# Stores of split weights, gates, x1, x2 and the output issued from GpSimd's queue instead of SyncE's

## The chip, the core and the metric

The kernel runs on one core of one Trainium2 chip. The metric is the device time in microseconds (us) of one execution. A core has TensorE (PE), VectorE (DVE), ScalarE (ACT), GpSimd (POOL) and SyncE (SP), each with its own instruction stream, and sixteen DMA engines that move data for whichever engine issues a transfer.

## The reference

Three residual sub-layers over x of shape 2 x 2048 x 1024 (float32), 4096 tokens in 32 tiles of 128:

```
x = x + 0.5 * ffn(layernorm(x))      # stage 1 (and the prep part of stage 2)
x = x + attn(layernorm(x))           # stage 2
x = x + 0.5 * ffn(layernorm(x))      # stage 3

attn: blocks of 128 tokens; scores of a block against itself and the block before it,
      masked, squared relu, times the values, times w_o
ffn:  thought = layer_norm(x[:, -1]) @ agg_w + agg_b            # last token of each batch only
      4 times: thought += gelu(layer_norm(thought) @ d1_w + d1_b) @ d2_w + d2_b
      broadcast = thought @ bc_w + bc_b
      gate = sigmoid(x @ gate_w + gate_b)                         # every token
      out  = layer_norm(x + gate * broadcast)
```

d1_w is 1024 x 4096 and d2_w 4096 x 1024, so each pass of the "thought" reads 32 MB of weights four times over for only two tokens. Each of the two ffn layers does so.

## The kernel before

All large products run as three float16 products of a high and a low half (a "split"). The order of all work is one list, `PLAN`, made by `whole_plan()`. Every engine has a program that walks the whole list and does its own part of each entry, so all five engines meet the entries in the same order, each at its own pace. An entry whose wait isn't met holds up all later entries on that engine, and only there.

- Stage 1 multiplies q and k weights and v and o weights together ("fold"), splits the gate weights, and computes the gates of all 32 tiles (`plan_gate`). Each gate tile ends in `gate_store`, a store of 512 KB into `gate1_dram` from a ring of 2 buffers, once ScalarE's sigmoid has raised `gated` (line 1356).
- Stage 2 computes x1 (`plan_prep`: norm, add the spread thought, norm, `x1_store` after `prep_stats`, then `prep_low` and the DMA transpose `group_turn`), then queries, values, scores and `collect`, which makes x2; `x2_stores` of a group come at the beginning of the next group's products.
- Stage 3 (`plan_stage_3`) computes gates and the second ffn for all tiles and ends each with `out_store`.
- The thought is a chain of small steps (`Thoughts`, `with_thought`) laid between the products of stage 1 and again of stage 2. Its weights come through ten buffers of 512 KB. `fetch_unit` (lines 836 to 845) issues the load of a unit once what was in the buffer is no longer needed. Some of the d1 and d2 units (64 in all, in both passes) are split into halves on the chip (`t_high` on ScalarE, `t_low` on VectorE, line 1843, which raises `unit_low`), stored to `parts_dram`, and read back from there in later steps (`pair` units).

All transfers are issued by SP. The loop of `sync_program` ends each thought entry with the fetches that hang on it:

```
elif kind == "t_low":
    _, n = a[0].info
    sp.wait_ge(unit_low, n + 1)
    sp.dma_start(parts_dram[...], unit_at(SPLITS[n].slot)).then_inc(parts_out[...], 16)
...
if kind[:2] == "t_":
    for n in a[0].fetch:
        fetch_unit(n)
```

`await_left` (lines 803 to 816), which `fetch_unit` calls, waits for `unit_low` of the same split where the buffer held a unit that was split, and for `unit_used`, raised by PE, in most other cases. POOL only computes the reciprocal square roots of the norms (`rstd`, line 1907, `normalisers`, line 1914) and of the thought (`t_var`, line 1945).

Transfers whose data is read again are guarded by completion semaphores: `x1_out` is waited for by `prep_fetch` (line 964) and `x1_fetch` (line 1002), `gate_out` by `prep_fetch` (line 968), `x2_out` by `x3` (line 1028), `parts_out` by `fetch_unit` and `t_high`, `out_out` by `x3` and the end of SP's program.

Of the kernel before, what the change touches and what calls it, by code (L numbers as in the profile page):

```python
# [14 lines left out]
P = 128  # L15
# [5 lines left out]
HALVES = D // BANK  # L21
# [19 lines left out]
TILE_OF = [b * NT + g * GROUP + i for b, g in GROUP_OF for i in range(GROUP)]  # L41
ORDER_3 = sorted(range(TILES), key=lambda tile: TILE_OF.index(tile) + 5 * (tile % GROUP == 0))
# [562 lines left out]
def macaron_kernel(nc, x, w_attn, w_o, in_gamma, in_beta, agg_w, agg_b, pn_gamma, pn_beta,  # L605
# [179 lines left out]
    def await_out(eng, key):  # L785

        at = BANK_AT[key]
        eng.wait_ge(product_out[at % PRODUCT_BANKS], at // PRODUCT_BANKS + 1)
# [42 lines left out]
    def sync_program():  # L831
# [15 lines left out]
        for kind, *a in PLAN:  # L847
# [56 lines left out]
            elif kind == "x":  # L904
# [3 lines left out]
                elif n:  # L908
                    sp.wait_ge(split_done, SPLIT_AT[("split", "gate", n - 1)] + 1)
                sp.dma_start(x_slots[n % X_RING], x_flat[row_of(TILE_OF[n]), :]).then_inc(x_in[n % X_RING], 16)  # L910
            elif kind == "gate_store":
                n, = a
                sp.wait_ge(gated, n * HALVES + 2)
                sp.dma_start(gate1_dram[row_of(TILE_OF[n]), :], gate_slots[n % GATE_RING]).then_inc(
                    gate_out[n % GATE_RING], 16)
            elif kind == "gate_save":
                k, = a
                sp.wait_ge(split_done, split_total("gate"))
# [4 lines left out]
            elif kind == "t_rows" and a[0].info[0] == 1:  # L923
# [3 lines left out]
                for b in range(B):  # L927
# [3 lines left out]
                    sp.dma_start(t_wide[b * KD:(b + 1) * KD, THOUGHT_ROWS * P:(THOUGHT_ROWS + 1) * P],  # L931
                                 xs_slots[c % XS_RING][P - 1:P, :].rearrange("o (k p) -> o k p", p=P)).then_inc(
                        rows_in, 16)
            elif kind == "t_low":
                _, n = a[0].info
                sp.wait_ge(unit_low, n + 1)
                sp.dma_start(parts_dram[n * P:(n + 1) * P, :], unit_at(SPLITS[n].slot)).then_inc(
                    parts_out[n % len(FOR_SPLITS)], 16)
            elif kind == "t_out":
                t, = a  # L940
                sp.wait_ge(t_dve, t.dve + 1)
                sp.dma_start(row_dram, t_wide[0:B * KD, 0:P]).then_inc(row_out, 16)
            elif kind == "publish":
                tau, = a
                sp.wait_ge(row_out, 16 * (tau + 1))
                if tau:
                    sp.wait_ge(gate_spread, TILES)
                else:
                    for slot in FOR_FIRST:
                        await_left(sp, THOUGHTS.taken[slot])  # L950
                sp.dma_start(thought_row[:, :, :].rearrange("p b d -> p (b d)"),
                             row_dram.rearrange("k p -> (k p)").partition_broadcast(P)).then_inc(thought_row_in, 16)
            elif kind == "prep_fetch":
                n, = a
                for u in (n * GROUP, n * GROUP + 1):
                    s = u % PREP_RING
                    if n == 0:
                        sp.wait_ge(fold_out[s], 16 * (2 * KD // FOLD_RING))
                        sp.wait_ge(split_done, split_total("vo"))
                    else:  # L960
                        sp.wait_ge(x1_out[s], 16 * (u // PREP_RING))
                        sp.wait_ge(h1_ready, u - PREP_RING + 1)
                        sp.wait_ge(y_made, u - PREP_RING + 1)
                    sp.dma_start(px_slots[s], x_flat[row_of(TILE_OF[u]), :]).then_inc(px_in[s], 16)  # L964
                    sp.wait_ge(gate_out[u % GATE_RING], 16 * (u // GATE_RING + 1))
                    if n:
                        sp.wait_ge(group_in[s], 16 * n)
                    sp.dma_start(pg_slots[s], gate1_dram[row_of(TILE_OF[u]), :]).then_inc(pg_in[s], 16)
            elif kind == "group_turn":
                u, = a  # L970
                n, i = divmod(u, GROUP)
                sp.wait_ge(lows_made, u + 1)
                if n >= 4:
                    sp.wait_ge(product_full, BANK_AT[("score", n - 2, 0)] + 1)
                elif n >= 2:
                    sp.wait_ge(product_full, BANK_AT[("gate", TILES - 1, 1)] + 1)
                    sp.wait_ge(gate_saved, 16 * KD)
                else:
                    for slot in FOR_SPLITS:
                        await_left(sp, last_split[0, slot])  # L980
                sp.dma_start_transpose(  # L981
                    group_of(n).rearrange("p h k t -> p (h k) t")[:, :, i * P:(i + 1) * P],
                    pg_slots[u % PREP_RING].bitcast(F16)).then_inc(group_in[i], 16)
            elif kind == "x1_store":
                u, = a
                sp.wait_ge(x1_made, u + 1)
                sp.dma_start(x1_dram[row_of(TILE_OF[u]), :], px_slots[u % PREP_RING]).then_inc(
                    x1_out[u % PREP_RING], 16)
            elif kind == "x1_fetch":
                c, = a  # L990
                s, u = c % XS_RING, COLLECTS[c][1]
                if c < XS_RING:
                    sp.wait_ge(product_full, BANK_AT[("gate", TILES - 1, 1)] + 1)
                    for i in range(GATE_RING):
                        sp.wait_ge(gate_out[i], 16 * len(range(i, TILES, GATE_RING)))
                else:
                    sp.wait_ge(x2_out[s], 16 * (c // XS_RING))
                    sp.wait_ge(moments_made, MOMENT_AT[("x2_stats", c - XS_RING)] + 1)
                    if c - XS_RING in LAST_TOKENS:
                        sp.wait_ge(rows_in, 16 * 2 * B)  # L1000
                sp.wait_ge(x1_out[u % PREP_RING], 16 * (u // PREP_RING + 1))
                sp.dma_start(xs_slots[s], x1_dram[row_of(TILE_OF[u]), :]).then_inc(xs_in[s], 16)
            elif kind == "x2_stores":
                n, = a
                for c, (at, u, _, _) in enumerate(COLLECTS):
                    if at == n:
                        await_out(sp, ("collect", c, 0))
                        await_out(sp, ("collect", c, 1))
                        sp.dma_start(x2_dram[row_of(TILE_OF[u]), :], xs_slots[c % XS_RING]).then_inc(
                            x2_out[c % XS_RING], 16)  # L1010
            elif kind == "load_3":

                sp.wait_ge(product_full, BANK_AT[("q", GROUPS - 1, KD - 2)] + 1)
                sp.wait_ge(gate_saved, 16 * KD)
                sp.dma_start(wide_a[:, :, :].rearrange("p k d -> p (k d)"), gate_pair_dram).then_inc(gate_loaded, 16)
                sp.wait_ge(product_full, BANK_AT[("score", GROUPS - 2, 0)] + 1)
                sp.dma_start(bias_3, gate_b.partition_broadcast(P)).then_inc(bias_in, 16)
            elif kind == "x3":
                n, = a
                s, c = n % X3_RING, COLLECT_OF[TILE_OF.index(ORDER_3[n])]  # L1020
                if n >= X3_RING:
                    sp.wait_ge(out_out[s], 16 * (n // X3_RING))
                elif n < PREP_RING:
                    sp.wait_ge(group_in[n], 16 * GROUPS)
                else:
                    sp.wait_ge(product_full, BANK_AT[("v", GROUPS - 1, 1, 1)] + 1)
                sp.wait_ge(x2_out[c % XS_RING], 16 * (c // XS_RING + 1))
                sp.dma_start(x3_slots[s], x2_dram[row_of(ORDER_3[n]), :]).then_inc(x3_in[s], 16)
            elif kind == "turn_3":
                n, = a  # L1030
                s = n % PAIR3_RING
                sp.wait_ge(lows3_made, n + 1)
                if n >= PAIR3_RING:
                    sp.wait_ge(product_full, BANK_AT[("gate_3", n - PAIR3_RING, 1)] + 1)
                else:
                    await_thoughts(sp)
                sp.dma_start_transpose(as_pair(pair3_slots[s]).rearrange("p h k t -> p (h k) t"),
                                       low3_slots[s].bitcast(F16)).then_inc(pair3_in[s], 16)
            elif kind == "out_store":
                n, = a  # L1040
                sp.wait_ge(ended_3, n + 1)
                sp.dma_start(out_flat[row_of(ORDER_3[n]), :], x3_slots[n % X3_RING]).then_inc(
                    out_out[n % X3_RING], 16)
            if kind[:2] == "t_":
                for n in a[0].fetch:
                    fetch_unit(n)
# [852 lines left out]
    def gpsimd_program():  # L1899
# [16 lines left out]
        for kind, *a in PLAN:  # L1916
            if kind == "start":
# [9 lines left out]
                pool.affine_select(out=identity[:, :], in_=identity[:, :], compare_op=ALU.not_equal, fill=1.0,  # L1927
                                   base=0, pattern=[[-1, P]], channel_multiplier=1).then_inc(constants, 1)
                pool.wait_ge(zeroed, 1)
            elif kind == "norm":  # L1930
                normalisers((kind, a[0]), token_stats[:, TILE_OF[a[0]], :])
            elif kind == "prep_y":
# [44 lines left out]
```

## Time and profile before

| | us |
|---|---|
| median of 3 runs | 2104.67 (2100.16 to 2111.58) |
| profiled execution, its own time | 2108.0 |
| its span, first to last instruction | 2106.8 |
| PE busy | 2012.4 (96%) |
| DVE busy | 1208.6 (57%) |
| ACT busy | 680.0 (32%) |
| POOL busy | 161.8 (8%) |
| mean busy share of the DMA queue that carries all data | 75.9% |

The profile lists busy time by engine, idle time before an instruction with what ended it, and for DMA instructions the time that they hold the issuing queue. "SPq" is SP's queue. TensorE's granted clock was 0.989 of full speed on average. The data moved is 555.78 MB.

### The profile page before, as it was taken

The page shows a single profiled execution, that of the slowest core. Times are in us where ns is not written, and L with a number is a line of the kernel's source. Part 1 is how long each engine was busy: PE and PEld are TensorE (multiplying, and loading weights), DVE is VectorE, ACT ScalarE, POOL GpSimd, SP SyncE. Part 2 cuts the span into 40 slices and gives each one's busy share as a digit, 9 for nine tenths or more (in the row PEclk, how much of TensorE's full clock was granted, in tenths as well). Part 3 has the DMA queues.
Part 4 walks back from the last instruction along what each step waited for, and adds up shares of the span by engine and source line. Part 5 has one row for each costly group of instructions (what it writes and reads, how often), then busy time and mean ns, then how long its engine had stood idle before and what let it go on. Part 6 is the DMA issues. An engine that isn't in the chain of part 4 may idle for free.

```text
span 2106.8 us, 30594 instructions
## 1 busy us (share of the span) xinstructions
PE 2012.4 (96%) x12010; PEld 1026.6 (49%) x12010; DVE 1208.6 (57%) x2152; ACT 680.0 (32%) x947; POOL 161.8 (8%) x278
## 2 busy tenths in 40 slices
PE   8999988998899999998999999999999999999997
PEld 3333433333333347655565556665556564444443
DVE  2323677223533465666766655655555545888887
ACT  0567445212323332223333222111212113444443
POOL 0000000000000010010000000000000001111111
PEclk9999999999999999999999999999999999999999
DMA  8689996878898843358989898898987947555552
GB/s 340 240 324 382 366 326 245 303 272 323 343 399 336 324 154 107 101 152 318 325 289 340 263 318 292 300 350 289 310 287 285 339 161 210 152 154 154 151 150 80
DMA packets 275214, 555.78 MB, mean 264 GB/s; under 512 B 149040, under 2 KB 149248, under 8 KB 274688
## 3 DMA queue, kind: packets, MB, share of 16 engines
q1 hardware_dynamic: 275072, 553.83, 75.9%
q8 instruction: 96, 1.57, 0.3%
q14 instruction: 46, 0.38, 0.0%
HBM read 406.93 MB, written 113.26 MB: 247 GB/s over the span
## 4 chain that ended last, share of the span: by engine, by line
PE 48%; DMA 3%; DVE 2%; SPq 1%; ACT 1%; issue 1%; POOL 0%; ACTq 0%; DVEq 0%
PE product_banks L1060 41%; PE product_banks L1195 3%; PE thought_acc L1260 3%; DMA thought_units<-parts_scratch 1%; DMA gate_arena<-arena 1%; DVE thought_units L1843 0%; SPq L845 0%; SPq L981 0%; DMA thought_units<-in_d_w 0%; PE thought_turn L1268 0%; ACT arena L1376 0%; ACT arena L1379 0%; PE thought_acc L1250 0%; DVE arena L1655 0%; SPq L964 0%
## 5 line engine op out<-in xcount | busy, mean ns | idle before, releaser
L1060 PE MATMUL product_banks<-gate_arena,arena 128*128 128x512 f16 x1536 | 359.3, 386 | 0.0
L1060 PE MATMUL product_banks<-wide_a,thought_units 128*128 128x512 f16 x1536 | 331.7, 379 | 0.0
L1060 PE MATMUL product_banks<-gate_arena,wide_a 128*128 128x256 f16 x2688 | 308.4, 275 | 3.2 <-DMA gate_arena<-arena 3.0
L1060 PE MATMUL product_banks<-wide_b,gate_arena 128*128 128x512 f16 x1344 | 301.8, 379 | 0.0
L1060 PEld LDWEIGHTS product_banks<-gate_arena,wide_a 128*128 128x128 f16 x2688 | 260.9, 99 | 60.6 <-issue 29.7
L1060 PEld LDWEIGHTS product_banks<-gate_arena,arena 128*128 128x128 f16 x1536 | 147.1, 99 | 206.1 <-issue 55.9
L1060 PEld LDWEIGHTS product_banks<-wide_a,thought_units 128*128 128x128 f16 x1536 | 150.3, 98 | 181.6 <-DVE arena L1695 0.3
L1060 PEld LDWEIGHTS product_banks<-wide_b,gate_arena 128*128 128x128 f16 x1344 | 127.1, 98 | 167.6 <-issue 24.9
L1484 DVE BATCH_NORM_STATS2 bn_parts<-arena 128x6 f32<-128x512 f32 x256 | 164.2, 683 | 4.4
L1907 POOL TENSOR_TENSOR token_stats<-stats,minus_half 128x1 f32<-128x1 f32 x96 | 65.7, 684 | 1039.9 <-DVE stats L1492 863.4
L1509 DVE SCALAR_TENSOR_TENSOR arena<-product_banks,inverse_gate,arena 128x512 f32<-128x512 f32 x64 | 47.8, 748 | 166.2 <-PE product_banks L1060 166.1
L1664 DVE SCALAR_TENSOR_TENSOR gate_arena<-product_banks,gate_arena 128x256 f16<-128x256 f32 x128 | 54.1, 423 | 144.5 <-ACT gate_arena L1391 142.2
L1092 PE MATMUL product_banks<-wide_a,wide_b 128*128 128x512 f32 x256 | 121.0, 614 | 6.1 <-DMA wide_a<-in_w_attn 6.0
L1397 ACT ACTIVATE arena<-product_banks,inverse_vo 128x512 f32<-128x512 f32 x64 | 44.0, 687 | 236.8 <-PE product_banks L1060 236.7
L1260 PE MATMUL thought_acc<-thought_units,thought_parts 128*6 128x512 f16 x1328 | 101.2, 381 | 19.9 <-DMA thought_units<-parts_scratch 13.7
L1195 PE MATMUL product_banks<-arena,key_weights 128*128 128x512 f32 x248 | 112.8, 600 | 6.9 <-issue 3.2
L1907 POOL TENSOR_TENSOR stats<-stats,minus_half 128x1 f32<-128x1 f32 x64 | 64.2, 1003 | 700.8 <-DVE stats L1492 416.3
L1368 ACT ACTIVATE arena<-arena,token_stats 128x1024 f32<-128x1024 f32 x32 | 39.5, 1236 | 230.7 <-DMA arena<-in_x 230.7
L1391 ACT ACTIVATE gate_arena<-product_banks 128x256 f16<-128x256 f32 x128 | 41.5, 379 | 211.5 <-PE product_banks L1060 211.5
L1425 ACT ACTIVATE arena<-arena 128x512 f32<-128x512 f32 x64 | 40.3, 630 | 175.5 <-DVE arena L1509 175.5
L1655 DVE SCALAR_TENSOR_TENSOR arena<-arena 128x1024 f16<-128x1024 f32 x32 | 39.2, 1224 | 96.3 <-ACT arena L1379 96.1
L1092 PEld LDWEIGHTS product_banks<-wide_a,wide_b 128*128 128x128 f32 x256 | 46.5, 193 | 71.0 <-issue 71.0
(206 smaller groups left out, 2278.5 us busy)
## 6 DMA issues: line engine op xcount, KB each, us to landing
thought_units<-parts_scratch SPq DMA_DIRECT2D x268, 512.0 KB, 5.9
thought_units<-in_d_w SPq DMA_DIRECT2D x164, 512.0 KB, 6.9
arena<-in_x SPq DMA_DIRECT2D x64, 512.0 KB, 8.5
parts_scratch<-thought_units SPq DMA_DIRECT2D x64, 512.0 KB, 6.0
x_scratch<-arena SPq DMA_DIRECT2D x64, 512.0 KB, 7.2
thought_row<-in_d_w SPq DMA_DIRECT2D x60, 512.0 KB, 6.9
arena<-x_scratch SPq DMA_DIRECT2D x40, 512.0 KB, 6.6
gate_scratch<-arena SPq DMA_DIRECT2D x32, 512.0 KB, 7.2
```

The costliest lines, as they stand in the source:

```text
L1060: mm = pe.matmul(bank, left(i, k), right(j, k), start=(n == 0), stop=(n == 3 * KD - 1))
L1092: mm = pe.matmul(bank_ap(key), wide_b[:, e, d * P:(d + 1) * P], wide_a[:, e, h * BANK:(h + 1) * BANK], start=(e == 0), stop=(e == KD - 1))
L1195: mm = pe.matmul(bank_ap(key), weights_of(u)[:, side, :], value_slot(other)[:, h * BANK:(h + 1) * BANK], start=(side == 0), stop=(side == ...
L1260: mm = pe.matmul(thought_acc[at:at + PARTS * B, :], value, unit[:, part, h * BANK:(h + 1) * BANK], start=first and part == 0, stop=last an ...
L1368: act.activation(ph_slots[u % PREP_RING], px_slots[u % PREP_RING], ACT.Identity, bias=st[:, 1:2], scale=st[:, 0:1]).then_inc(h0_made, 1)
L1391: act.activation(queries[:, query_place(n * GROUP + i), 0, e - 1:e + 1, :], made[:, i], ACT.Copy, scale=QUERY_SCALE).then_inc(q_high_made, 1)
L1397: act.activation(value_slot(n * GROUP + i)[:, h * BANK:(h + 1) * BANK], bank_ap(key), ACT.Copy, scale=inverse["vo"][:, :]).then_inc(out_of ...
L1425: act.activation(res, res, ACT.Sigmoid).then_inc(gated_3, 1)
L1484: dve.bn_stats(bn_parts[:, h, :], source[:, h * BANK:(h + 1) * BANK]).then_inc(own.up(), 1)
L1509: dve.scalar_tensor_tensor(out=res[:, cols], in0=bank_ap(key), scalar=inverse["gate"][:, :], in1=bias[:, cols], op0=ALU.mult, op1=ALU.add) ...
L1664: low = dve.scalar_tensor_tensor(out=q[:, 1], in0=made[:, i], scalar=QUERY_SCALE, in1=q[:, 0], op0=ALU.mult, op1=ALU.subtract)
L1907: return pool.tensor_tensor(to, st[:, 2:3], minus_half[:, 0:1], ALU.pow)
```

## The change

Five kinds of entry move from `sync_program` to `gpsimd_program`, with the same waits, the same data and the same semaphores: `gate_store` (32 stores), `t_low` (64), `x1_store` (32), `x2_stores` (32) and `out_store` (32), 192 stores of 512 KB each. They stand at the same places of PLAN. The other stores (`fold_store`, `gate_save`, `t_out`), all loads and all transposes stay on SP, as do the fetches that hang on a `t_low` entry and the final wait for `out_out`.

```diff
-            elif kind == "gate_store":            # in sync_program
-                n, = a
-                sp.wait_ge(gated, n * HALVES + 2)
-                sp.dma_start(gate1_dram[row_of(TILE_OF[n]), :], gate_slots[n % GATE_RING]).then_inc(
-                    gate_out[n % GATE_RING], 16)
...
+            elif kind == "gate_store":            # in gpsimd_program
+                n, = a
+                pool.wait_ge(gated, n * HALVES + 2)
+                pool.dma_start(gate1_dram[row_of(TILE_OF[n]), :], gate_slots[n % GATE_RING]).then_inc(
+                    gate_out[n % GATE_RING], 16)
+            elif kind == "t_low":
+                _, n = a[0].info
+                pool.wait_ge(unit_low, n + 1)
+                pool.dma_start(parts_dram[n * P:(n + 1) * P, :], unit_at(SPLITS[n].slot)).then_inc(
+                    parts_out[n % len(FOR_SPLITS)], 16)
+            elif kind == "x1_store":
+                u, = a
+                pool.wait_ge(x1_made, u + 1)
+                pool.dma_start(x1_dram[row_of(TILE_OF[u]), :], px_slots[u % PREP_RING]).then_inc(
+                    x1_out[u % PREP_RING], 16)
+            elif kind == "x2_stores":
+                n, = a
+                for c, (at, u, _, _) in enumerate(COLLECTS):
+                    if at == n:
+                        await_out(pool, ("collect", c, 0))
+                        await_out(pool, ("collect", c, 1))
+                        pool.dma_start(x2_dram[row_of(TILE_OF[u]), :], xs_slots[c % XS_RING]).then_inc(
+                            x2_out[c % XS_RING], 16)
+            elif kind == "out_store":
+                n, = a
+                pool.wait_ge(ended_3, n + 1)
+                pool.dma_start(out_flat[row_of(ORDER_3[n]), :], x3_slots[n % X3_RING]).then_inc(
+                    out_out[n % X3_RING], 16)
```

## Rows read from the trace of the kernel before

**Rows 1.** Busy time by stretch: PE, PEld, DVE, ACT, POOL, PEclk, DMA share, GB/s.
```profile
0.00:700.00 700.00, 642.98 (x3296) 257.92 (x3297) 289.58 (x562) 275.55 (x393) 34.88 (x72) 0.98 0.86 324
900.00:1200.00 300.00, 283.50 (x1918) 168.00 (x1917) 204.78 (x380) 93.53 (x118) 24.84 (x48) 0.98 0.85 285
1200.00:1764.00 564.00, 561.84 (x4025) 332.70 (x4024) 308.73 (x635) 110.69 (x169) 36.70 (x90) 1.00 0.85 289
1764.00:2106.80 342.80, 331.49 (x1536) 150.10 (x1534) 288.00 (x362) 143.53 (x186) 49.66 (x36) 0.99 0.53 146
```

**Rows 2.** Waits of PE: for what, us in total, times, longest.
```profile
PE thought_acc L1250 <- DMA thought_units<-in_d_w: 18.7, 14, 3.3
PE thought_acc L1260 <- DMA thought_units<-parts_scratch: 13.7, 7, 5.7
PE thought_acc L1250 <- DMA thought_row<-in_d_w: 5.4, 6, 2.7
PE product_banks L1060 <- DMA gate_arena<-arena: 3.0, 2, 2.4
```

**Rows 3.** Waits of SP's queue, same columns.
```profile
SPq L845 <- PE thought_acc L1260: 369.9, 119, 17.0
SPq L937 <- DVE thought_units L1843: 121.4, 45, 8.0
SPq L987 <- DVE arena L1645: 121.1, 16, 19.0
SPq L914 <- ACT arena L1356: 28.7, 5, 11.3
```

**Rows 4.** Timeline of SP's queue ahead of PE's longest DMA wait: start, us held.
```profile
945.36 0.33 SPq L937 DMA_DIRECT2D parts_scratch<-thought_units  x1
945.73 0.43 SPq L845 DMA_DIRECT2D thought_units<-in_d_w  x1
...
951.94 0.86 SPq L1009 DMA_DIRECT2D x_scratch<-arena  x2
952.89 0.92 SPq L845 DMA_DIRECT2D thought_units<-parts_scratch  x2
```

**Rows 5.** Timeline of PE: the unit before, and its two longest waits after 900 us.
```profile
948.25 0.60 PE L1260 MATMUL thought_acc<-thought_units,thought_parts 128*6 128x512 f16 x8
...
965.83 1.02 PE L1260 MATMUL thought_acc<-thought_units,thought_parts 128*6 128x512 f16 x8 [5.75 <-DMA thought_units<-parts_scratch]
...
1142.83 0.60 PE L1260 MATMUL thought_acc<-thought_units,thought_parts 128*6 128x512 f16 x8
...
1157.94 1.02 PE L1260 MATMUL thought_acc<-thought_units,thought_parts 128*6 128x512 f16 x8 [3.28 <-DMA thought_units<-parts_scratch]
```

**Rows 6.** Timeline of SP's queue ahead of the second of them.
```profile
1142.25 1.97 SPq L1009 DMA_DIRECT2D x_scratch<-arena  x2
1144.31 0.86 SPq L845 DMA_DIRECT2D thought_units<-parts_scratch  x2
```

**Rows 7.** Chain of work that ended last: start us, us, what.
```profile
953.42 12.27 DMA thought_units<-parts_scratch
...
1144.78 13.02 DMA thought_units<-parts_scratch
```

**Rows 8.** Busy time in the stretch where the DMA engines are fullest (columns of Rows 1).
```profile
200.00:300.00 100.00, 89.33 (x501) 41.89 (x500) 73.14 (x130) 47.57 (x62) 7.01 (x13) 0.97 0.95 360
```

**Rows 9.** DMA issues: KB each, median us from issue to landing.
```profile
thought_units<-parts_scratch SPq DMA_DIRECT2D x268, 512.0 KB, 5.9
thought_units<-in_d_w SPq DMA_DIRECT2D x164, 512.0 KB, 6.9
```

**Rows 10.** POOL's instructions, by line (busy us, mean ns, idle before).
```profile
L1907 POOL TENSOR_TENSOR token_stats<-stats,minus_half 128x1 f32<-128x1 f32 x96 | 65.7, 684 | 1039.9 <-DVE stats L1492 863.4 <-DVE stats L1494 176.5
```

**Rows 11.** The same from 1764 us on.
```profile
L1907 POOL TENSOR_TENSOR stats<-stats,minus_half 128x1 f32<-128x1 f32 x32 | 46.8, 1461 | 284.5 <-DVE stats L1734 284.5
```

**Rows 12.** DVE, grouped: the only wide one-input TENSOR_SCALAR from SBUF (x2 in all).
```profile
L1590 DVE TENSOR_SCALAR half_beta<-half_beta 128x1024 f32<-128x1024 f32 x1 | 0.7, 685 | 0.0
```

**Rows 13.** Timeline of the last twenty microseconds: DVE's last, and SP's last three stores.
```profile
2084.73 19.72 SPq L1042 DMA_DIRECT2D out<-wide_b  x3
2102.80 1.28 DVE L1751 SCALAR_TENSOR_TENSOR wide_b<-arena,stats,wide_b 128x1024 f32<-128x1024 f32 x1 [0.49 <-DVE arena L1746]
```

**Rows 14.** Line 1042, the stores of the output: ns min, median, max; then to landing.
```profile
L1042 SPq DMA_DIRECT2D out<-wide_b x24: 332/337/343, 1805.0 to 2104.1; - x24
...
DMA to landing us min/median/max: 2.6/2.9/4.6
```

More of the change, by code:

```diff
@@ L933, in sync_program @@
                         rows_in, 16)
[L934 to L938, printed above, removed]
             elif kind == "t_out":
@@ L983, in sync_program @@
                     pg_slots[u % PREP_RING].bitcast(F16)).then_inc(group_in[i], 16)
[L984 to L988, printed above, removed]
             elif kind == "x1_fetch":
@@ L1002, in sync_program @@
                 sp.dma_start(xs_slots[s], x1_dram[row_of(TILE_OF[u]), :]).then_inc(xs_in[s], 16)
[L1003 to L1010, printed above, removed]
             elif kind == "load_3":
@@ L1038, in sync_program @@
                                        low3_slots[s].bitcast(F16)).then_inc(pair3_in[s], 16)
[L1039 to L1043, printed above, removed]
             if kind[:2] == "t_":
```

## The prediction

> **What bounds the kernel now.** I read the busy time by stretch first. From 1200 us to the end PE is busy 561.8 of 564.0 us and then 331.5 of 342.8 us, and the missing 11 us of the last stretch are the tail after its last product [rows 1]. In that half no store can be made to matter, wherever it is issued, unless something new stops PE. Before it PE idles 57 us up to 700 us and 16.5 us between 900 and 1200 us [rows 1]. PE's own waits say for what: 18.7 + 13.7 + 5.4 us for units of the thought's weights to land and 3.0 us for a transpose, 40.8 us in 29 waits [rows 2]. That is all that transfers cost on the bounding engine beside the start, and so the most that a better SP queue could give back.
>
> The next view is the waits of SP's queue. Its largest is line 845, a fetch that waits until PE has finished with a buffer, 369.9 us [rows 3]. This isn't touched. The entries that move away held SP for 121.4 us (line 937, `t_low`), 121.1 us (line 987, `x1_store`) and 28.7 us (line 914, `gate_store`) [rows 3]. It looks like 271 us of a blocked queue, but most of it is not removed.
>
> **Part 1, `t_low` (64 stores).** The wait is for `unit_low` of the split. The next thing SP does is a fetch into the buffer that this split has just read, and `await_left` waits for the same count. The timeline shows the pair: store at 945.36 held 0.33 us, fetch at 945.73 [rows 4]. When the store leaves, the 121.4 us of waiting move from line 937 to the fetch on line 845, and only the 0.33 us of issue is saved, 64 times, 21 us of SP's time that SP mostly has to spare. Value for the path: nothing by itself; it counts where SP runs late, which is priced in part 3.
>
> **Part 2, `x1_store`, `gate_store`, `out_store`.** After `x1_store` SP's next fixed stop is `group_turn`, which needs the low half made from x1, later than x1 itself. Only thought fetches that lie between the two get free. After 1200 us and in stage 3 PE has no wait that they could shorten [rows 1, 2]. `gate_store` blocks only 5 times, 28.7 us [rows 3]. I count 1 us for the fetches behind these, of bounds 0 and the 29 us that PE waits for units before 700 us (all of rows 2 but the two waits of rows 5 and the transpose: 18.7 + 13.7 + 5.4 - 5.75 - 3.28 = 28.8).
>
> **Part 3, `x2_stores`, the clearest gain.** PE's two longest waits for a unit are 5.75 us at 965.83 and 3.28 us at 1157.94 [rows 5]. Each time the unit before had ended on PE at 948.85 and 1143.43 (948.25 + 0.60, 1142.83 + 0.60) [rows 5], but SP issued the pair of fetches only at 952.89 and 1144.31, behind two x2 stores that held it 0.86 and 1.97 us [rows 4, 6]. The fetches then took 12.27 and 13.02 us to land [rows 7] against a median of 5.9 us [rows 9], since these stores and the loads of the next group stand ahead of them. Two stores are 1.05 MB, at 360 GB/s 2.9 us of all engines [rows 8]. With the stores gone from SP's queue the fetch is issued up to 0.86 us earlier (at the second place the buffer frees only 0.88 us before the issue) and no longer stands behind all of them, but the engines still have to move them: I take half of 2.9 us. That is 0.86 + 1.45 = 2.3 us at each place, 4.6 us, of bounds 0 (POOL issues the stores at the same moment and they take as much) and 9.0 us (both waits gone). The transpose wait (2.4 of the 3.0 us in one piece) gains one issue, 0.4 us.
>
> **Part 4, what POOL now does.** The trace has no DMA issued from POOL. The nearest rows are SP's issue of the same store, 0.34 us [rows 14], and POOL's own one-column instruction, 0.68 us on average and 1.46 us in stage 3 [rows 10, 11]. I take 1.0 us, between these: 192 us in all on an engine that is busy 8%. Behind a waiting store on POOL stand the reciprocal roots of later norms. They wait for VectorE instructions later in PLAN anyway (POOL's first group idles 1039.9 us for DVE [rows 10]), so a store that waits for VectorE delays them by its issue only; `gated` comes from ScalarE, but for a tile whose sigmoid is an entry back. `x1_store` now stands behind `normalisers` of its own tile, so it starts some 3.5 us later (two statistics and two POOL instructions), at worst 0 to 2 us of SP waiting for `x1_out` in stage 2, where PE has a stock. I cost these at 0; if the cover went, 32 tiles by 1 us.
>
> **Part 5, the tail.** The last `out_store` is on the path. Today DVE ends at 2104.08, the store is issued in 0.34 us and lands 2.6 us later, which ends the span [rows 13, 14]. With POOL's issue at 1.0 us, and at most 1.5, the tail grows by 0.7 to 1.2 us, and by up to 2 if the landing nears the longest of the output's, 4.6 us; I take 1.2 us. The Trainium skill (DMA: Bandwidth & Descriptors, section Latency and other measured facts) gives about 1 us to the first byte for a transfer issued from GpSimd against 0.6 us from SyncE; by it alone the tail would grow by 0.4 us. No row here shows it.
>
> **Part 6, sharing.** The stretch from 200 to 300 us has the engines 95% busy at 360 GB/s [rows 8]. Two queues then share them. What a fetch gains by not standing behind a store it loses when the store is served beside it. I take 1 us of loss, bounds -3 and +25.
>
> A rule that speaks against the change is weighed here. The two-input DVE instructions run beside POOL's roots in stage 3, and these take 1.46 us in place of 0.68 [rows 10, 11], so the two engines do hinder one another. The Trainium skill (SBUF — State Buffer, section SBUF: two separate sides) says that GpSimd can't write descriptors while VectorE runs a two-port copy or tensor_scalar. By that rule little changes here: wide instructions of that kind from SBUF are two of 0.68 us in the whole trace [rows 12]. Were two-input instructions to block too, each issue in stage 3 might take 1.3 us more; it is in the second rival.
>
> **Sum.** Gains 4.6 + 0.4 + 1.0 = 6.0 us, losses 1.2 + 1.0 = 2.2 us, net -3.8 us on the profiled execution's 2108.0 us (span 2106.8 and 1.2 around it), 2104.2. The median of the runs shown is 2104.67, 3.3 us under the profiled one, so I state 2104.67 - 3.8 = 2100.9, as 2101 us, 0.2% below. Within 0.5% (10.5 us) a measurement can't tell from no change.
>
> **Rivals.**
> - *Nothing but the tail.* Part 3 gives 0, since POOL issues x2 stores at the same moment and the engines serve them first. For it: SP's wait moves to line 845 in part 1 in the same way. Then +1.2 and +1: 2106.9. Chance 0.25.
> - *Slower: the second queue delays fetches.* Place: 100 to 700 us. There PE waits 29 us for units, with the engines near full. 57 stores (32 of split units, 25 of gates) now go beside the loads; each takes 1.5 us (0.52 MB at 360 GB/s). If half of them push one fetch by 1.5 us and PE sees half of this: 57 x 0.5 x 1.5 x 0.5 = 21 us, 2122 to 2128. It decides if the median time to landing of fetches rises by over 1 us from 5.9 and 6.9 [rows 9]. Against it: the bytes are the same. To it I add a POOL issue so slow (over 3 us) or so hindering that stage 3 suffers: VectorE has (342.8 - 288.0) / 32 = 1.7 us per tile free [rows 1]; beyond it each us costs 32. Chance 0.23 for both, 0.17 for the first.
> - *Faster by more.* All stores out of the way shorten half of the 40.8 us of waits [rows 2]: -20 us, 2085. For it: any late fetch is late at once on PE. Against it: before 700 us SP mostly waits for PE itself at line 845, thus isn't late. Chance 0.14.
>
> **How the numbers follow.** The forecast has 0.38 (2096 to 2106). Forecast and first rival lie within 0.5%, less 0.03 for a larger gain: same 0.60. Faster 0.14 + 0.03 = 0.17, slower 0.23. The range reaches from 2089 (forecast and the upper bound of part 3 with some of part 2) to 2124 (first slower rival).
>
> **What would show it.** Waits of SP: line 937 and 987 gone, and line 845 on DVE line 1843 near 120 us in its place, else part 1 is wrong. PE's waits near 966 and 1158 us shorter by about 2 us each, the fetches ahead landing in under 12 us (part 3). POOL's queue holding each store for about 1 us (part 4). The last store landing 1 us later after DVE's last (part 5). Medians to landing of unit fetches within 0.5 us (part 6). The forecast is wrong if PE's waits for units before 700 us grow above 35 us, or PE shows new waits after 1200 us.

## The result, and the profile after

The changed kernel takes 2120.53 us (median of 6 runs, 2110.98 to 2129.68), beside 2104.56 us of the kernel before (6 runs): ratio 1.0077 with a 95% interval of 1.0044 to 1.011. It is 0.77% slower, 16 us; the prediction said 2101 us and most likely faster by a hair. Its profiled execution took 2124.09 us with a span of 2122.8, against 2108.0 and 2106.8.

The page of the kernel after, its first section and its DMA queues and issues. Line numbers change with the edit: 1250 is now 1222, 1260 is 1232, 1060 is 1032.

```profile
PE 2020.8 (95%) x12010; PEld 1029.9 (49%) x12010; DVE 1208.9 (57%) x2152; ACT 680.4 (32%) x947; POOL 274.7 (13%) x470
...
q1 hardware_dynamic: 247424, 453.15, 63.1%
q0 software_dynamic: 27648, 100.68, 12.0%
...
thought_units<-parts_scratch SPq DMA_DIRECT2D x268, 512.0 KB, 6.0
thought_units<-in_d_w SPq DMA_DIRECT2D x164, 512.0 KB, 6.9
...
parts_scratch<-thought_units POOLq DMA_DIRECT2D x64, 512.0 KB, 7.3
x_scratch<-arena POOLq DMA_DIRECT2D x64, 512.0 KB, 6.1
thought_row<-in_d_w SPq DMA_DIRECT2D x60, 512.0 KB, 7.2
```

There is a second queue, q0, with 100.68 MB. PE did the same 12010 products, but was busy 8.4 us longer (2020.8 against 2012.4): some of them ran at a lower clock. The medians to landing are those of [rows 9], 6.0 for 5.9 and 6.9 for 6.9 us. A median over 430 fetches doesn't show the loss; a stretch of time does. Windows of the kernel after (columns of [rows 1]):

```profile
0.00:700.00 700.00, 637.49 (x3221) 255.03 (x3221) 283.21 (x552) 274.50 (x390) 66.24 (x126) 0.97 0.85 317
900.00:1200.00 300.00, 285.16 (x1964) 172.97 (x1963) 204.57 (x367) 92.35 (x121) 53.36 (x97) 0.98 0.82 279
1780.00:2122.80 342.80, 330.93 (x1534) 149.80 (x1531) 287.92 (x362) 143.52 (x186) 69.88 (x71) 0.99 0.51 145
200.00:300.00 100.00, 90.66 (x483) 41.19 (x481) 67.38 (x123) 40.53 (x54) 17.58 (x32) 0.92 0.90 325
```

From 200 to 300 us PE gets through 483 instructions where it did 501 [rows 8], at a granted clock of 0.92 and not 0.97; the last stretch is as it was. Setting each product of the one trace beside the same product of the other places the loss. The table says how many us later than before the product starts that before started at the time on top; in each trace time is counted here from its first product, which starts 6.0 us (before) and 5.9 us (after) into the span.

```
us in before    94   194   246   295   395   596   795   1298  1757  2089
after         -0.5  +4.3  +9.5 +11.4 +11.8 +14.4 +14.7  +15.3 +14.5 +15.5
```

11 of the 15.5 us are lost between 180 and 300 us, 3 more up to 600 us, and less than 1 us from 800 us to the end. Waits of PE from 60 to 760 us, in the kernel after and then before (what for: us in total, times, longest):

```profile
PE thought_acc L1222 <- DMA thought_units<-in_d_w: 22.6, 17, 4.1
PE thought_acc L1222 <- DMA thought_row<-in_d_w: 8.2, 5, 3.3
PE turn_banks L1041 <- DVE arena L1473: 7.4, 4, 4.0
PE thought_acc L1232 <- DMA thought_units<-parts_scratch: 4.7, 4, 1.8
```
```profile
PE thought_acc L1260 <- DMA thought_units<-parts_scratch: 4.7, 5, 2.2
```

Waits for units of the thought's weights grow by 3.9 + 2.8 us over [rows 2]; all waits of PE in this stretch from 52.5 to 59.6, by 7.1 us. The rest is clock: PE's busy time for the same products grew by 8.4 us. 7.1 + 8.4 = 15.5, which is the lag to be explained. (Over the whole span PE idles 94.4 us before and 102.0 after, 7.6 more, and 7.6 + 8.4 are the 16.0 us of the span.) The granted clock bears this out: PE was busy at half speed (1.2 GHz) for 35.9 us of the trace before and 53.0 after, 17.1 us more, and half of this is 8.6 us. From 190 to 300 us the half speed lasted 6.2 us before and 17.1 after.

How one wait arises: two timelines of the kernel after, SP's queue and then POOL, and under them SP's queue of the kernel before (start, us held).

```profile
246.39 0.94 SPq L845 DMA_DIRECT2D thought_units<-in_d_w  x2
247.38 1.83 SPq L845 DMA_DIRECT2D thought_row<-in_d_w  x2
```
```profile
243.04 0.60 POOL L1910 DMA_DIRECT2D parts_scratch<-thought_units  x1
246.94 0.53 POOL L1910 DMA_DIRECT2D parts_scratch<-thought_units  x1 [3.31 <-DVE thought_units L1815]
247.47 0.53 POOL L1905 DMA_DIRECT2D gate_scratch<-arena  x1
248.13 0.53 POOL L1910 DMA_DIRECT2D parts_scratch<-thought_units  x1
```
```profile
242.16 0.81 SPq L845 DMA_DIRECT2D thought_units<-in_d_w  x2
243.02 0.44 SPq L937 DMA_DIRECT2D parts_scratch<-thought_units  x1
243.50 0.45 SPq L845 DMA_DIRECT2D thought_row<-in_d_w  x1
243.99 1.11 SPq L914 DMA_DIRECT2D gate_scratch<-arena  x1
```

And when these same transfers had all their data landed, worked out from the landing events of each trace:

```
before (all SP)                     after
issued  what           landed       issued  queue what           landed
242.16  unit           248.87       246.39  SP    unit           255.61
242.53  unit           250.12       246.77  SP    unit           258.09
243.02  split store    251.41       246.94  POOL  split store    254.33
243.50  thought row    252.60       247.38  SP    thought row    259.94
243.99  gate store     253.93       247.47  POOL  gate store     256.80
245.15  split store    255.13       248.13  POOL  split store    259.30
```

Before, one queue lands them in the order of issue, one each 1.2 to 1.3 us, and the gate store comes after the pair of units. After, two stores issued behind the pair land before its second unit, and the unit takes 11.32 us in place of 7.59. This gate store is not an early one: it leaves 6.8 us behind its tile's second sigmoid, and 7.5 in before. What changed for it is the queue. PE waits for just this unit. Timeline of PE after (first the wait of 190 to 200 us, then this one), and before:

```profile
198.17 1.04 PE L1222 MATMUL thought_acc<-thought_row,narrow_hidden 128*6 128x512 f32 x8 [2.19 <-DMA thought_row<-in_d_w]
...
258.22 1.89 PE L1222 MATMUL thought_acc<-thought_units,narrow_in 128*6 128x512 f32 x8 [4.13 <-DMA thought_units<-in_d_w]
```
```profile
195.65 1.04 PE L1250 MATMUL thought_acc<-thought_row,narrow_hidden 128*6 128x512 f32 x8
...
250.26 1.04 PE L1250 MATMUL thought_acc<-thought_units,narrow_in 128*6 128x512 f32 x8 [0.40 <-DMA thought_units<-in_d_w]
```

The start moves by 8.0 us: 4.2 since the fetch is issued later (246.77 - 242.53, PE being late already), 3.7 since it takes longer. Then the eight products take 1.89 us where they took 1.04. Windows after, and before:

```profile
250.00:260.00 10.00, 5.87 (x36) 2.06 (x34) 7.99 (x12) 4.71 (x6) 0.76 (x2) 0.86 1.02 417
260.00:270.00 10.00, 10.00 (x46) 3.87 (x43) 5.69 (x7) 2.74 (x4) 1.66 (x3) 0.80 0.82 262
```
```profile
250.00:260.00 10.00, 9.74 (x54) 3.91 (x55) 9.90 (x14) 4.79 (x6) 0.73 (x2) 1.00 1.02 413
260.00:270.00 10.00, 8.07 (x46) 3.64 (x43) 9.90 (x16) 2.23 (x4) 0.28 (x1) 1.00 1.02 371
```

PE was busy 5.87 of the ten us in which the clock fell, and 9.74 in before, where it didn't; from 260 to 270 us it is busy all the time and does 46 products at 0.80. The first wait (at 198 us) does come from an early store: the first gate store leaves POOL at 186.23 us, ahead of the row's fetch (188.64); before, SP issued it at 194.41, behind this fetch and five others of the thought's weights. The fetch lands in 9.40 us and not 7.02.

### The profile page after: what moved, and what is told of

It is laid out like the page before. It is cut to its first block and busy times, and to the rows that moved or that the text cites. A ratio compares the mean times of both kernels' runs of the same rounds, so it can differ in the third digit from the quotient of the medians.

```text
span 2122.8 us, 30594 instructions
## 1 busy us (share of the span) xinstructions
PE 2020.8 (95%) x12010; PEld 1029.9 (49%) x12010; DVE 1208.9 (57%) x2152; ACT 680.4 (32%) x947; POOL 274.7 (13%) x470
## 3 DMA queue, kind: packets, MB, share of 16 engines
q0 software_dynamic: 27648, 100.68, 12.0%
## 5 line engine op out<-in xcount | busy, mean ns | idle before, releaser
L1032 PE MATMUL product_banks<-gate_arena,arena 128*128 128x512 f16 x1536 | 366.2, 391 | 0.0
```

The costliest lines, as they stand in the source:

```text
L1032: mm = pe.matmul(bank, left(i, k), right(j, k), start=(n == 0), stop=(n == 3 * KD - 1))
```

## The experiments

Ratios are to the kernel before, run on the same chip in the same rounds, with the 95% interval.

### Which stores: one kind at a time

Each kernel moves the entries named and leaves all others on SP. For the gates (`e1_gate`):

```diff
-            elif kind == "gate_store":        # sync_program
-                sp.wait_ge(gated, n * HALVES + 2)
-                sp.dma_start(gate1_dram[...], gate_slots[...]).then_inc(...)
...
+            elif kind == "gate_store":        # gpsimd_program
+                pool.wait_ge(gated, n * HALVES + 2)
+                pool.dma_start(gate1_dram[...], gate_slots[...]).then_inc(...)
```

Gates alone: 

> Only the 32 gate stores leave SP for POOL. Sharing theory (a store on a second queue is served beside fetches that were issued before it, so these land late, PE waits, and the clock drops to half after the wait): in the changed kernel the first step of the lag, 4 us at 195 to 200 us, comes ahead of any store of split weights and so from a gate store; expected +3 to +7 us, with PE's wait for thought_row at about 196 us present. Rival (the loss is in the stores of split weights alone): within 2 us of before.

`t_low` alone (`e2_parts`): 

> Only the 64 stores of split weights leave SP for POOL. Sharing theory: the 4.1 us wait of PE at 254 us in the changed kernel had two such stores and one gate store beside the late fetches; expected +4 to +10 us, lag gathered between 210 and 400 us. Rival (gate stores do it all, by being issued up to 8 us earlier): within 2 us of before.

`x1_store`, `x2_stores` and `out_store` (`e3_late`): 

> x1, x2 and output stores leave SP for POOL, nothing in stage 1. Sharing theory as now read: the lag of the changed kernel (15.5 us) is there by 300 us but for 3 us, so this kernel has -3 to +3 us against before. Rival (POOL's issue or its hold on VectorE costs in stages 2 and 3): +5 us or more, with PE waiting for VectorE after 1200 us. My prediction's part 3: -4 us, with shorter waits of PE near 966 and 1158 us.

Measured: gates 2120.45 us, 1.0075 (1.0055 to 1.0095); `t_low` 2106.68, 1.0011 (0.9996 to 1.0027); the late ones 2108.16, 1.0015 (0.9999 to 1.0032). The 32 gate stores, a sixth of those moved, are enough for the whole loss. That the 64 split stores would carry it fell: they cost nothing that can be told from nothing. Both sizes were missed: the gates cost 16 us where 3 to 7 were expected, the split stores 2 us where 4 to 10 were. PE's first waits from 60 to 760 us and the window from 190 to 300 us, gates alone:

```profile
PE thought_acc L1245 <- DMA thought_units<-in_d_w: 25.2, 16, 3.3
PE thought_acc L1245 <- DMA thought_row<-in_d_w: 7.6, 5, 3.8
```
```profile
190.00:300.00 110.00, 100.57 (x549) 45.57 (x545) 70.25 (x127) 51.03 (x70) 10.73 (x19) 0.94 0.93 343
```

It is after's loss: +7.4 us at 295, +12.3 at 596, +14.5 at the end, half speed for 13.7 us from 190 to 300. Why gates and not splits: the split's store is the entry ahead of the fetch that it frees the buffer for, so SP issued it as early as POOL does; the gate store stood behind fetches. From the end of a tile's second sigmoid to the issue of its store pass 6.9 us on SP on average (tiles 2 to 25), 3.1 on POOL here. In the whole change it is 4.7, since gate stores there also queue behind split stores on POOL.

The late stores answer for the prediction's part 3. Timelines of POOL, SP's queue and PE in that kernel, at PE's longest wait after 900 us:

```profile
951.43 1.13 POOL L1923 DMA_DIRECT2D x_scratch<-arena  x2 [0.28 <-issue]
```
```profile
953.69 1.40 SPq L845 DMA_DIRECT2D thought_units<-parts_scratch  x2
```
```profile
967.31 1.02 PE L1242 MATMUL thought_acc<-thought_units,thought_parts 128*6 128x512 f16 x8 [5.90 <-DMA thought_units<-parts_scratch]
```

The x2 stores leave SP, and the pair behind them is issued only 0.5 us earlier: 7.01 us after the split store that is issued at 946.68 here, 7.53 us after the same store at 945.36 in before [rows 4]. The pair takes 12.23 and 12.77 us (11.57 and 12.27 before), and PE waits 5.90 us where it waited 5.75 [rows 5]. This profiled execution took 2117.36 us, the longest of its twelve.

### Whose queue, and how early

`e4_gate_act`: the same entry at the same place of PLAN, issued by ScalarE, whose own work orders it. 

> The 32 gate stores leave SP for ScalarE's queue, which is of the same kind as SP's. If any second queue does the harm (sharing), the time is that of the kernel with the gate stores on POOL, +3 to +7 us. If the cause is how POOL makes its transfers, it is within 2 us of before while the POOL version isn't.

```diff
+            elif kind == "gate_store":        # scalar_program, removed from sync_program
+                act.wait_ge(gated, n * HALVES + 2)
+                act.dma_start(gate1_dram[...], gate_slots[...]).then_inc(...)
```

Measured: 2104.99 us, 1.0009 (0.9994 to 1.0023). There ScalarE reaches the store 6.1 us after the sigmoid, about as late as SP. The window from 190 to 300 us is about before's. Before, then ScalarE:

```profile
190.00:300.00 110.00, 99.33 (x565) 46.31 (x558) 75.00 (x133) 55.26 (x76) 7.01 (x13) 0.97 0.96 362
```
```profile
190.00:300.00 110.00, 98.96 (x568) 45.54 (x566) 74.46 (x132) 55.70 (x78) 7.01 (x13) 0.98 0.97 365
```

A second queue for these 32 stores thus costs nothing by itself. Two kernels change how early the store is issued: on POOL it waits for the first sigmoid of the next tile as well (`e5_pool_late`), and on ScalarE it is issued at once (`e6_act_early`).

```diff
-                pool.wait_ge(gated, n * HALVES + 2)          # e5_pool_late, on gates alone
+                pool.wait_ge(gated, (n + 1) * HALVES + 1 if n + 1 < TILES else n * HALVES + 2)
...
+                if h == 1:                                   # e6_act_early, behind the sigmoid
+                    act.wait_ge(gated, n * HALVES + 2)
+                    act.dma_start(gate1_dram[...], gate_slots[...]).then_inc(...)
```

> Gate stores alone on POOL, as in the run that lost 0.75%, but each waits also for the first sigmoid of the next tile, so it starts about when ScalarE's queue started it (some 6 us after its gate is ready, where POOL alone did so after some 3). Theory (the harm is the early start: SP's order kept these stores behind fetches that PE needs first): back within 4 us of before. Rival (the harm is POOL's kind of queue): still +12 us or more.

> Gate stores on ScalarE's queue, issued at once after the tile's second sigmoid and not half a tile later. Theory (early start does the harm on any queue): +8 to +16 us, though the same queue cost nothing when the stores were issued later. Rival (only POOL's queue does harm): within 3 us of before.

Measured: late on POOL 2109.77 us, 1.0024 (1.0006 to 1.0041); at once on ScalarE 2113.06, 1.0035 (1.0018 to 1.0052). The delay takes 0.5 points from POOL's loss, and the earliness brings 0.26 to ScalarE. Neither meets its forecast in full: on POOL 5 us remain, between the 4 of the theory and the 12 of the rival, and ScalarE loses 7 us where 8 to 16 were expected. Nor was the delay on POOL what was meant: the late store leaves POOL 8.3 us behind the sigmoid and not some 6, later than on SP, and VectorE once waits 3.6 us for a gate buffer to be stored, which it doesn't in before; the store at once leaves ScalarE 0.03 us behind it, earlier than POOL's 3.1. ScalarE's window falls to:

```profile
190.00:300.00 110.00, 98.34 (x546) 44.99 (x543) 72.34 (x128) 51.79 (x72) 7.02 (x13) 0.95 0.94 348
```

`e7_first_early` is `e5_pool_late` with tile 0 issued at once, `e12_rest_early` the opposite: tile 0 late, all others at once.

```diff
+                pool.wait_ge(gated, (n + 1) * HALVES + 1 if 0 < n < TILES - 1 else n * HALVES + 2)  # e7
+                pool.wait_ge(gated, (n + 1) * HALVES + 1 if n == 0 else n * HALVES + 2)             # e12
```

> As the delayed version on POOL, but the very first gate store (tile 0, at about 186 us) starts at once. The traces show 3.6 to 4.3 us of lag gathered around it. Theory: +3 to +6 us against before, all of it by 200 us and in the clock's next half-speed stretches. Rival (each store costs a little, none stands out): no different from the fully delayed version.

> Gate stores on POOL, only tile 0's delayed, all others at once: the complement of the run with only tile 0's early (+0.41%). With all early it was +0.75%, with all delayed +0.24%. If the first store is the one that matters: +0.2 to +0.35%. If every early store adds: +0.5 to +0.7%.

Measured: 2111.46 us, 1.0041 (1.0021 to 1.0061), and 2112.88, 1.0039 (1.0024 to 1.0054), where none early has 1.0024 and all early 1.0075. So it isn't the first store alone: over none early, the first alone adds 0.17 points and all the others 0.15, both together 0.51, which their intervals can't tell from the sum. The first came out above its +3 to +6 us (9 us, of 4 to 13), the second between its two forecasts. In the profiles the first store's wait is there with e7 (+9.2 us at 295) and gone with e5 (-0.1), a larger step than the medians of whole runs bear out; one profiled execution is one draw.

`e8_all_late` is the whole change with the gate stores delayed as in e5. 

> The whole change, all 192 stores on POOL, with the gate stores delayed in the same way. Theory: the change without its harm, within 5 us of before (stores of split weights +2, later stores +4 by their own runs, hardly told from nothing). Rival (POOL's queue as such): as the whole change, +16 us.

Measured: 2113.59 us, 1.0044 (1.0018 to 1.0069): part of the loss comes back, no gain appears. That is 9 us, over the 5 of the theory and under the 16 of the rival. The losses of its parts, 0.24 + 0.11 + 0.15 points, add up to about as much. `e11_sp_later` tries the other direction, on SP as in before but at the end of the tile's entries:

```diff
-                if n:
-                    out.append(("gate_store", n - 1))   # inside the tile's entries
+    if n:
+        out.append(("gate_store", n - 1))               # behind all of them
```

> All on SP as before, but a gate store stands at the end of the tile's entries, two thirds of half a tile later. If later is always better: -2 to -5 us against before. If the present place is late enough: within 2 us. Rival (a store too late holds up the ring of two gate buffers): slower, with VectorE waiting for the gate store and PE for VectorE.

Measured: 2113.82 us, 1.0045 (1.003 to 1.0061). VectorE now waits for the two-buffer ring to be stored, a wait that before doesn't show:

```profile
DVE arena L1509 <- DMA gate_scratch<-arena: 20.0, 7, 4.5
```

PE's longest wait for VectorE's line 1509 grows from 3.2 to 5.3 us and its waits for thought rows from 5.4 to 7.8; that the ring makes the whole 10 us is not shown. So the place on SP's queue was the best of those tried: earlier, on another queue, the store is served beside fetches that PE is about to need, and later it holds its buffer longer. An earlier place on SP's own queue was not tried.

### Bytes or the queue itself

Four kernels store 16 of a gate tile's 128 rows, an eighth of the bytes, and load tiles of x in stage 2 in place of the gates; the computation is changed by that. `e10_sp_small` has the store on SP, `e9_pool_small` on POOL, `e13_act_small` on ScalarE at once, `e14_pool_small_late` on POOL with e5's delay.

```diff
-                sp.dma_start(gate1_dram[row_of(TILE_OF[n]), :], gate_slots[n % GATE_RING])...
+                sp.dma_start(gate1_dram[row_of(TILE_OF[n]), :][0:16, :], gate_slots[n % GATE_RING][0:16, :])...
...
-                    sp.dma_start(pg_slots[s], gate1_dram[row_of(TILE_OF[u]), :]).then_inc(pg_in[s], 16)
+                    sp.dma_start(pg_slots[s], x_flat[row_of(TILE_OF[u]), :]).then_inc(pg_in[s], 16)
```

> Gate stores stay on SP, but each moves 16 of 128 rows (64 KB, an eighth), and the loads of gates in stage 2 read tiles of x instead, as many bytes; so 7/8 of the gates' store traffic is left out. It is the control for the same on POOL. If store bytes ahead of fetches cost in stage 1 even in SP's order: -3 to -8 us. If they cost nothing there: within 2 us.

> The same small gate stores, but on POOL and issued early, as where all the bytes cost 0.75%. Theory (the bytes served beside fetches do the harm): same time as the control on SP, within 3 us. Rival (POOL's issue or its queue itself slows something): 6 us or more slower than the control.

> Leaves out work as the two small-store kernels do: of each gate tile 16 of 128 rows are stored, and stage 2 loads tiles of x in place of the gates. The small store is issued by ScalarE right behind the tile's second sigmoid, so as early as on POOL's queue or earlier, but not by POOL. The same stores on SP gave 0.9958 of before, on POOL (early) 0.9983. Theory 'it is the earliness': this kernel is as slow as the POOL one, 0.998 (0.997 to 0.9995). Rival 'it is POOL's queue itself': as fast as the SP one, 0.996 (0.9945 to 0.997).

> Leaves out the same work. The small store on POOL's queue, but behind the first sigmoid of the next tile. Theory 'it is the earliness': as fast as the stores on SP, 0.996 (0.9945 to 0.997). Rival 'it is POOL's queue itself': 0.998 (0.997 to 0.9995).

Measured, beside the same placement with all the bytes:

```
                    512 KB stores                    64 KB stores
SP, in order        1 (before)                       0.9958 (0.9943 to 0.9973)
POOL, early         1.0075 (1.0055 to 1.0095)        0.9983 (0.9971 to 0.9995)
POOL, late          1.0024 (1.0006 to 1.0041)        0.9953 (0.9935 to 0.9971)
ScalarE, at once    1.0035 (1.0018 to 1.0052)        0.9946 (0.9930 to 0.9963)
```

With few bytes, issuing at once costs nothing on ScalarE (0.9946 against SP's 0.9958), and POOL's queue costs nothing when its stores are late (0.9953). So `e13_act_small` speaks against the earliness alone, and `e14_pool_small_late` against POOL's queue alone. With all the bytes, issuing at once costs 0.35% on ScalarE. What the bytes cost follows from the table, column against column: 0.42 points on SP in order, 0.71 on POOL late, 0.89 on ScalarE at once and 0.92 on POOL early. Issued early on a second queue the same bytes cost 0.47 (ScalarE) and 0.50 points (POOL) more than in SP's order. Each of these two is uncertain by some 0.3 points, but they agree and both stand clear of nothing: this part is the bytes of a store beside earlier fetches. It is two thirds of POOL's 0.75. The other 0.25 points are there with small stores too (0.9983 against 0.9958), and neither reason alone gives them; I expected at most 3 us and it is 4 to 5.

## Why the prediction was wrong

**Part 1** (the wait goes to the fetch) was right. Waits of SP's queue after:

```profile
SPq L845 <- PE thought_acc L1232: 429.7, 121, 17.0
...
SPq L971 <- DVE arena L1627: 234.7, 27, 27.3
...
SPq L845 <- DVE thought_units L1815: 142.8, 48, 9.3
```

The 121.4 us of line 937 [rows 3] have become 142.8 us on line 845, and the wait of `x1_store` stands at line 971, `group_turn`: SP wasn't freed, it waits for the same things elsewhere.

**Part 6, sharing, is the step that failed, and with it what part 2 says of the gate stores.** Part 6 put 1.0 us of loss into the sum (of bounds -3 and +25), and part 2 gave the gate stores a share of 1 us of gain, since they block SP only 28.7 us [rows 3]. Moved alone, the gate stores cost 16 us (1.0075). The prediction read the queue for what SP waits for and not for the order in which it serves: a store that stands behind fetches is held back by them. Part 6 then said that what a fetch gains by not standing behind a store it loses beside it. The runs agree for a store that stood ahead of the fetch (`t_low`, 1.0011). They don't for one that stood behind: that fetch had nothing to gain, and the second queue puts part of the store's bytes before it. While both queues are loaded they get packets about one for one: with gates alone on POOL, from 191 to 192 us, SP's queue started 51 packets of 4096 bytes and POOL's 55; with gates late on ScalarE, from 200 to 201 us, 51 and 52. The Trainium skill (DMA: Bandwidth & Descriptors, section Queues, rings and completion order) says that a DMA engine goes round its queues packet by packet; the nearly equal shares agree with that. The same page (section Issuing engines are not separate DMA queues) says that initiating from several engines "will only save the time on the sequencer"; here SP's 0.33 us or more for each store was saved and the kernel lost 0.77%. The measurement decides: the saving isn't all that a second queue does.

**The price** was off for a second reason. No term of the sum had the clock; it makes 8.4 of the 16 us. That the lower clock follows from the waits is argued from when it falls (the windows above) and not shown: no run held the clock fixed. The half-speed time from 190 to 300 us goes with the loss only roughly. It was 6.2 us before, 3.9 with gates late on ScalarE, 9.1 late on POOL, and 10.2, 13.7 and 17.1 with gates early on ScalarE, early on POOL, and after; but it was 9.5 with only the late stores moved, where stage 1 is that of before, and 6.8 in the whole change with late gates, which is 0.44% slower. One profiled execution for each kernel leaves some 3 us to chance here.

**Part 3** was wrong, 4.6 us that didn't come: the rival "nothing but the tail" had it, POOL issues the x2 stores at the same moment and they are served ahead. With only the late stores moved PE's waits for `parts_scratch` stay at 9.1 us. After, from 900 to 1320 us, they are one of 5.0 us (before 9.0 in two, [rows 5]), but those for the transposes rise from 2.4 to 4.6 us and a new one of 1.7 us for VectorE ends at 1295 us. It is one of the signs the prediction named, a new wait of PE after 1200 us. In the kernel with only the late stores moved it is 3.8 us; there two x2 stores are issued behind the four loads of the next group; the first lands before all four of them, the second before two.

**Part 4**: POOL's issue costs less than the 1.0 us taken. Lines of POOL after:

```profile
L1910 POOL DMA_DIRECT2D parts_scratch<-thought_units x64 | 35.1, 548 | 208.8 <-DVE thought_units L1815 205.5 <-issue 3.0
L1905 POOL DMA_DIRECT2D gate_scratch<-arena x32 | 18.5, 579 | 7.8 <-ACT arena L1328 7.2
```

0.55 to 0.60 us each; that it is hidden was right: less than 1 us is lost after 800 us, and stage 3 is unhurt.

**Part 5**: the tail. DVE's last ended 2.7 us before the span's end in before and 3.2 us in after (2118.27 + 1.29 = 2119.56 of 2122.8), +0.5 and not +1.2 us. Timeline after:

```profile
2118.27 1.29 DVE L1723 SCALAR_TENSOR_TENSOR wide_b<-arena,stats,wide_b 128x1024 f32<-128x1024 f32 x1 [0.52 <-DVE arena L1718]
2119.85 0.58 POOL L1928 DMA_DIRECT2D out<-wide_b  x1 [1.67 <-DVE wide_b L1723]
```

**The rivals.** The slower one had the mechanism and the place (100 to 700 us), with a chance of 0.17. That it had the size as well (2122 us and more) is luck: its sum counts 57 stores, of which the 32 of split units cost nothing that shows, and it has no term for the clock. What spoke against it, "the bytes are the same", is no reason: the bytes are the same and their order isn't. Its test was useless, though. It was to decide by a median to landing over 1 us higher; the medians stayed, and the other test, PE's waits for units before 700 us over 35 us, is what rose, from 28.8 to 35.5 us (22.6 + 8.2 + 4.7, above, up to 715 us, where the work lies that before did by 700; up to 700 us it is 34.4). A handful of fetches in the full stretch carry it. The range held the time, the likeliest case's own didn't.

**Open.** POOL loses more than ScalarE for the same gate stores when they are early: 1.0075 against 1.0035 with all the bytes, 0.9983 against 0.9946 with few. How early they are doesn't explain it, since ScalarE's leave 3 us before POOL's. Late ones have 1.0024 against 1.0009, which overlap, and POOL's leave 2 us later there; late small stores show no such rest. What in POOL's early stores makes these 0.4 points isn't settled; packets of 4096 bytes take 0.159 us in the median on either queue.

## What to carry to other kernels

A single in-order queue is also a priority list: before a store is moved to a queue of its own, list what is issued ahead of it and who waits for that, for these are the transfers that it will overtake. The stores that stood just ahead of the fetch they free a buffer for could be moved here without a gain or loss that shows; the stores that stood behind urgent fetches, in a stretch where the DMA engines are 95% busy, were best left there. Look for the loss by stretch and by single wait, not by medians, and put the clock into the price of a wait on TensorE.

## What the runs showed of the hardware

- One queue that is backed up lands 512 KB transfers in the order of issue, one each 1.2 to 1.3 us (242 to 256 us, before). Two that are backed up share the packets about one for one (51 and 55 in one us), and an earlier fetch on the one took 11.32 us and not 7.59.
- The issue of a 512 KB store holds SP for 0.33 to 0.43 us in the median, by kind of store, and up to 1.5 us in single cases; it holds POOL for 0.53 to 0.74 us. Where nothing of its own was ahead of it, the first packet came at best 1.1 us after the issue from POOL and 0.8 us from ScalarE; for gate stores between 180 and 700 us up to 4.9 and 4.5 us.
- In the changed kernel TensorE's granted clock fell from 2.4 to 1.2 GHz around the wait of 4.13 us that ended at 258 us (0.86 on average from 250 to 260 us, where PE was busy 5.87 us) and was 0.80 on average from 260 to 270 us, where PE was busy all the time. With 7.6 us more of idle time on PE in the whole trace came 17.1 us more of busy time at 1.2 GHz.
